# Local attention of a four-layer recurrent network: 1/sqrt as exp of minus half a logarithm, value projections and the next row's shift placed earlier in a step

## The reference, cut to what matters

```
h = shift_token(x)
q, k, v = split(h @ wqkv)
q = l2norm(q) * qs
k = l2norm(k) * ksc
q, k = rotary_xpos(q, k)
o = local_attention(q, k, v)
x = x + o @ wo
```

## Time and profile before

| | us |
|---|---|
| median of 3 runs | 2914.24 |
| lowest, highest | 2912.70, 2918.39 |
| the profiled execution, its time | 2911.34 |
| its span in the trace | 2909.5 |
| PE busy | 2305.2 (79%) |
| DVE busy | 1535.6 (53%) |
| ACT busy | 1138.6 (39%) |
| POOL busy | 637.8 (22%) |
| mean granted TensorE clock | 0.885 |

### The profile page before, as it was taken

The page is one execution under the profiler, slowest core; times in us unless marked ns, Lnnn a source line. Parts: engine busy times, 40 slices in busy tenths (PEclk is TensorE's granted clock), DMA queues, the critical chain, the costliest instruction groups (busy, mean ns, idle before and its releaser), DMA issues. The chain is left out here.

```text
span 2909.5 us, 54198 instructions
## 1 busy us (share of the span) xinstructions
PE 2305.2 (79%) x18107; PEld 1476.4 (51%) x18108; DVE 1535.6 (53%) x5386; ACT 1138.6 (39%) x1810; POOL 637.8 (22%) x689
## 2 busy tenths in 40 slices
PE   4487999997699999784888828447888866999997
PEld 1133777773267777431444416324554313777775
DVE  4635666635466665435677313147775245565663
ACT  5623554433244544333555402133554340233333
POOL 0204434300244342002010040421110012221210
PEclk8796999998899999896999869767999865899999
DMA  2000000000000000001222140202221002333330
GB/s 109 0 0 1 1 1 0 0 1 0 0 1 2 0 0 1 1 4 45 70 80 67 55 150 0 62 28 81 73 74 33 0 33 90 92 111 91 91 110 30
DMA packets 81241, 115.82 MB, mean 40 GB/s; under 512 B 10352, under 2 KB 67184, under 8 KB 77720
## 3 DMA queue, kind: packets, MB, share of 16 engines
q1 hardware_dynamic: 79024, 109.48, 12.4%
q0 software_dynamic: 2048, 4.20, 0.5%
HBM read 69.70 MB, written 42.86 MB: 39 GB/s over the span
## 5 line engine op out<-in xcount | busy, mean ns | idle before, releaser
L1240 ACT ACTIVATE at_pr<-ps 128x768 f32<-128x768 f32 x384 | 312.1, 813 | 505.7 <-PE ps L1176 505.7
L1282 DVE CUSTOM_DVE_ANT_0 at_junk<-ps,conf 128x128 f32<-128x128 f32 x768 | 220.1, 287 | 235.7 <-PE ps L1158 216.0
L1284 DVE CUSTOM_DVE_ANT_0 at_junk<-ps,conf 128x256 f32<-128x256 f32 x768 | 321.4, 419 | 0.0
L1158 PE MATMUL ps<-at_ks,at_qs 40*128 40x128 f32 (+5 forms) x2048 | 223.0, 321 | 70.7 <-DVE at_m L1284 26.9
L1170 PE MATMUL ps<-at_qs,at_ks 41*128 41x256 f32 (+5 forms) x2048 | 199.5, 294 | 58.2 <-DMA at_qs<-at_ml 28.4
L693 POOL TENSOR_TENSOR la_tc<-la_ta,la_tb 128x512 f32<-128x512 f32 x128 | 162.3, 1268 | 354.6 <-DVE la_tb L959 354.6
L710 PE MATMUL ps<-w_l0f,la_hs 128*128 128x512 f32 x256 | 152.5, 680 | 54.4 <-POOL la_hs L675 36.3
L1170 PEld LDWEIGHTS ps<-at_qs,at_ks 41*128 41x128 f32 (+2 forms) x2048 | 140.9, 145 | 105.9 <-ACT at_pr L1240 53.5
L860 ACT ACTIVATE la_pr<-ps 128x640 f32<-128x640 f32 x128 | 90.2, 705 | 265.8 <-PE ps L762 265.4
L1191 PE MATMUL ps<-at_pr,at_v 128*32 128x256 f32 (+1 forms) x3072 | 175.8, 341 | 16.4 <-issue 15.7
L1158 PEld LDWEIGHTS ps<-at_ks,at_qs 40*128 40x128 f32 (+2 forms) x2048 | 104.9, 151 | 160.3 <-DVE at_m L1284 59.2
(11 more groups left out here) (308 smaller groups left out, 4995.6 us busy)
## 6 DMA issues: line engine op xcount, KB each, us to landing
scratch_latent<-at_parts SPq DMA_DIRECT2D x32, 640.0 KB, 4.8
at_qs<-scratch_latent SPq DMA_DIRECT2D x32, 320.0 KB
at_ks<-scratch_latent SPq DMA_DIRECT2D x32, 320.0 KB
scratch_alibi<-at_parts SPq DMA_DIRECT2D x32, 192.0 KB, 2.3
at_ks<-scratch_alibi SPq DMA_DIRECT2D x192, 32.0 KB
scratch_rope<-at_parts SPq DMA_DIRECT2D x32, 192.0 KB, 2.3
at_ks<-scratch_rope SPq DMA_DIRECT2D x192, 32.0 KB
moe_weights<-in_moe SPq DMA_DIRECT2D x1, 4096.0 KB, 20.7
```

The lines of the kernel that those rows point to most:

```text
L1158: m = nc.tensor.matmul(o[:, cols:cols + keys], q[:, block_q:block_q + P], kk[:, 0:keys], start=True, stop=True)
L1240: nc.scalar.activation(pr[:, p % RING, :, :], ps[:, 6:8, 0:384], ACT.Exp, scale=scale).then_inc(s.at_prob, 1)
L1282: nc.vector.tensor_tensor_reduce(junk[:, x % 2, e, 0:P], ps[:, m + e, 0:P], k.cf("late")[:, P:2 * P], 1.0, BIG, ALU.add, ALU.max, m2[:, r, ...
L1284: last_max = nc.vector.tensor_tensor_reduce(junk[:, x % 2, e, P:3 * P], ps[:, m + e, P:3 * P], k.cf("late"), 1.0, BIG, ALU.add, ALU.max, m ...
```

## The change

`y1`, the first estimate of 1/sqrt(vc), is no longer one Abs_reciprocal_sqrt but two activations on ACT in the same place: Ln of `vc` into a new tile `lv`, then Exp with scale -0.5, which waits for the Ln. In each step, `project_values` runs in quarters 0 and 1, and `turn` in quarters 2 and 3, on PE, with ACT's copies out of bank 2 and the semaphore counts to match. `shift_in` of the next row runs on POOL in quarter 2. DVE's part is unchanged.

```diff
@@ -645,6 +645,7 @@
         qn = sb("qn", [P, 2, TILE])
         ss = sb("ss", [P, 4, H8])
         vc = sb("vc", [P, 4, H8])
+        lv = sb("lv", [P, 4, H8])
         y1 = sb("y1", [P, 4, H8])
         y2 = sb("y2", [P, 4, H8])
         rn = sb("rn", [P, 4, H8])
@@ -692,7 +693,7 @@
                         pool.wait_ge(s.la_rot, u + 1)
                         nc.gpsimd.tensor_tensor(tc[:, x, :], ta[:, x % 2, :], tb[:, x % 2, :], ALU.add).then_inc(s.la_tc, 1)
                         pool.wait_ge(s.la_tc, u + 1)
-                    if live(i, -1) and x == 3:
+                    if live(i, -1) and x == 2:
                         if live(i, 2):
                             pool.wait_ge(s.la_vprod, 2 * (row0 + i - 1))
                         shift_in(i + 1, (n + 1) % NS)
@@ -778,7 +779,8 @@
                 m.then_inc(s.la_attended, 1)
 
             def project_values(i, n, t):
-                at_least(pe, s.la_turned, 2 * (row0 + done(i - 1, 4)) + (1 if t and live(i, 4) else 0))
+                at_least(pe, s.la_turned, 2 * (row0 + done(i - 1, 4)))
+                at_least(pe, s.la_vread, 2 * (row0 + i - 2) + t)
                 pe.nop(nofuse=True)
                 nc.tensor.matmul(ps[:, 2, :], hs[:, n, t * P:(t + 1) * P], w("wv"), start=True, stop=True
                                  ).then_inc(s.la_vprod, 1)
@@ -786,7 +788,7 @@
             def turn(i, half):
                 b = row0 + i - 4
                 pe.wait_ge(s.la_divided, 4 * b + 2 * (half + 1))
-                at_least(pe, s.la_vread, 2 * (row0 + done(i - 1, 2)) + (half + 1 if live(i, 2) else 0))
+                at_least(pe, s.la_vread, 2 * (row0 + done(i, 2)))
                 at_least(pe, s.la_turned, 2 * b + half)
                 pe.nop(nofuse=True)
                 for c in range(2):
@@ -831,10 +833,10 @@
                         columns_of(i - row1, (x - 1) % 4)
                     if live(i, 0):
                         product(i, n, x)
-                    if live(i, 2) and x in (0, 2):
-                        project_values(i, (n - 2) % NS, x // 2)
-                    if live(i, 4) and x in (1, 3):
-                        turn(i, x // 2)
+                    if live(i, 2) and x in (0, 1):
+                        project_values(i, (n - 2) % NS, x)
+                    if live(i, 4) and x in (2, 3):
+                        turn(i, x - 2)
                     row = 3 + (x < 3)
                     if live(i, row):
                         values(i - row, (n - row) % NS, (x - 3) % 4)
@@ -861,7 +863,9 @@
                                              ).then_inc(s.la_prob, 1)
                     if live(i, 1) and x == 0:
                         act.wait_ge(s.la_clamped, b)
-                        nc.scalar.activation(y1[:], vc[:], ACT.Abs_reciprocal_sqrt).then_inc(s.la_rsqrt, 1)
+                        nc.scalar.activation(lv[:], vc[:], ACT.Ln).then_inc(s.la_ln, 1)
+                        act.wait_ge(s.la_ln, b)
+                        nc.scalar.activation(y1[:], lv[:], ACT.Exp, scale=-0.5).then_inc(s.la_rsqrt, 1)
                     row1 = 1 + (x < 1)
                     if live(i, row1):
                         p = (x - 1) % 4
@@ -876,14 +880,14 @@
                         act.wait_ge(s.la_product, 4 * b + x + 1)
                         at_least(act, s.la_ss, 4 * b + x - 1)
                         nc.scalar.activation(sq[:, x % 2, :], ps[:, 0, :], ACT.Square).then_inc(s.la_squared, 1)
-                    if live(i, 2) and x in (0, 2):
-                        act.wait_ge(s.la_vprod, 2 * (b - 2) + x // 2 + 1)
+                    if live(i, 2) and x in (0, 1):
+                        act.wait_ge(s.la_vprod, 2 * (b - 2) + x + 1)
                         if live(i, 2 + NS):
                             at_least(act, s.la_attended, HP8 * (b - 1 - NS))
-                        nc.scalar.copy(V[:, (n - 2) % NS, x // 2, :, 0:D64], heads(ps[:, 2, :])).then_inc(s.la_vread, 1)
-                    if live(i, 4) and x in (1, 3):
-                        c = x - 1
-                        act.wait_ge(s.la_turn, 2 * (b - 4) + x // 2 + 1)
+                        nc.scalar.copy(V[:, (n - 2) % NS, x, :, 0:D64], heads(ps[:, 2, :])).then_inc(s.la_vread, 1)
+                    if live(i, 4) and x in (2, 3):
+                        c = 2 * (x - 2)
+                        act.wait_ge(s.la_turn, 2 * (b - 4) + x - 1)
                         at_least(act, s.la_out, b - 4)
                         nc.scalar.copy(oT[:, c:c + 2, :].rearrange("p c t -> p (c t)"), ps[:, 2, :]).then_inc(s.la_turned, 1)
                     if live(i, 3) and x == 1:
@@ -2009,6 +2013,7 @@
         self.la_rot = new("la_rot")
         self.la_tc = new("la_tc")
         self.la_clamped = new("la_clamped")
+        self.la_ln = new("la_ln")
         self.la_rsqrt = new("la_rsqrt")
         self.la_norm = new("la_norm")
         self.la_qn = new("la_qn")
```

## The result

| | before | after |
|---|---|---|
| median, us | 2913.47 (4 runs) | 3008.55 (4 runs) |
| lowest to highest | 2911.65 to 2918.39 | 3007.27 to 3012.20 |
| profiled execution | 2911.34 | 3007.91 |
| its span | 2909.5 | 3006.1 |
| mean granted clock | 0.885 | 0.871 |

The ratio is 1.0326, with a 95% interval of 1.0308 to 1.0344: slower, by 95 us. The forecast had the sign and the mechanism, but 2974 us and a range up to 3000; the measured time lies 8.6 us above the range.

The account below looks back on a forecast made before the run. A step was taken as PE's work plus its waits, with ACT's chain through `y1` on the path in quarter 0. 2911.3 + 40 - 4 + 25 = 2972, with half of a 2.9 us median offset 2974 us; range 2944 to 3000.

Parts of the forecast that it names:

- Part one, Ln and Exp: ACT in quarter 0: two table loads ahead of `y1` make the chain 1.54 us longer in 26 steps, +40.0 us.
- What is saved in quarter 1: ACT's table load ahead of the exp of quarter 1 goes away, but it was hidden, so it gives nothing.
- Part two: POOL's shift in quarter 2: 0 in steady steps, 0.7 us gained at each of six starts, -4 us.
- Part three: Bank 2's order, projection and turn changing quarters on PE: 0, bounds -0.24 to +0.5 us a step.
- The clock: PE's quarter-0 stall of 2.5 us lowers the clock in 6 of 10 steps, 1.6 us each: +25 us, at most +42.
- The third rival: Two loads in quarter 0, and the clock falls in nearly every step and for longer: 2990 to 3030 us, chance 0.10.

Follow-up runs that it names:

- e2: The kernel before with only Ln and Exp in place of Abs_reciprocal_sqrt: 3004.22 us, ratio 1.0305 against the kernel before.
- e4: The changed kernel with eleven unused matmuls added on PE ahead of its wait for `la_ot`: 2960.07 us, ratio 1.0139 against the kernel before.
- e1: The changed kernel with Abs_reciprocal_sqrt back in place of Ln and Exp: 2915.49 us, ratio 1.0006 against the kernel before.
- e3: The changed kernel with one table set holding Ln and Exp loaded ahead of each local attention: 2870.03 us, ratio 0.9833 against the kernel before.
- e6: The changed kernel with Abs_reciprocal_sqrt back and DVE's quarter-0 divide ahead of the inverse norms: 2861.80 us, ratio 0.9838 against the kernel before.
- e8: The kernel before with only DVE's quarter-0 divide moved ahead of the inverse norms: 2886.37 us, ratio 0.9898 against the kernel before.
- e5: The changed kernel, Ln and Exp kept, with DVE's quarter-0 divide ahead of the inverse norms: 2900.26 us, ratio 0.9948 against the kernel before.

## Why the prediction was wrong in its size

By its own steps:

- **Part one, Ln and Exp: right.** Two loads ahead of `y1`, 32 under each line, 1.54 us longer, 26 steps. Where the clock held, the steps show this term by itself: 26.39 and 26.47 us in two steps of e2, 26.3 to 26.4 in e4, as the sum had them. 26 x 1.54 = 40 us stands.
- **What is saved in quarter 1: right**, nothing: e2 without a fall is those 1.54 us longer although the load of quarter 1 is gone.
- **Part two, -4 us: near.** From the first square to the first steady exp the changed kernel took 67.5 and 68.2 us, before 69.8 and 68.1: 2 us less in all. The shift's effect on the stall was under-priced: PE's product now runs on from the transposes, so the projection ended 0.7 us earlier and not 0.44, and the stall is 2.8 us where I had 2.5.
- **Part three, 0: right as far as the runs show.** e1 has the new order of bank 2 and the earlier shift, and its steps without a fall are as long as before. The two parts were tried only together.
- **The clock, +25 us: this step failed.** Between the first and the last quarter-0 exp of the two applications the changed kernel took 404.4 and 399.7 us, before 351.6 and 351.7, 100.8 more; 40 of it is part one, 61 the clock. The term was `26 x 0.6 x 1.6`, and both factors were too small. The share of stalls with a fall was 26 of 26, not 6 of 10: I had set one stall of 2.35 us against one of 2.15, two single stalls of which neither comes back in each step; e1 had the second one again and the clock fell there. And a fall costs 1.7 us only in 15 of 26: in 11 the clock stayed at 0.50 for 6.8 us instead of 3.4, and the step grew by 3.3. 15 x 1.7 + 11 x 3.3 = 62. My upper bound of +42, "all, at 1.6", wasn't one. The third rival, a fall in nearly every step and for longer, is what happened; I had given it 0.10 and cut the range at 3000 inside it.

Sum with what was measured: 2911.3 + 40 + 61 - 2 = 3010, beside 3007.9.

The Trainium skill's rule on the load ("ScalarE: Activation LUTs", table sets: ln then exp in one load) is true of the chip here and false of this program: one set does serve both, as e3 shows, but the loads that the build places by itself didn't choose it. The trace of before had said so in the earlier trace rows.

## What to carry to other kernels

Before swapping an activation for others "of the same table", look in the trace what the build loads for such a pair, and place the shared set by hand if it doesn't; then count the loads again. Ask which wait an in-order engine puts between two chains that have nothing to do with each other: here DVE's divide stood behind `y1` without reading it, and with the two blocks exchanged one load a row no longer costs anything that shows (e6, e8), and a second load costs 1.0 us a step (means of 24.36 in e5 and 23.33 in e6) where in the old order it cost 3.9 (28.80 in the changed kernel, 24.87 before). And where a change lengthens a stall of PE that comes back every step, price the clock as the worse case for all of them. Here that would have been 3.3 us for each of the 26, 86 us, where 61 were lost.

## What the runs showed of the hardware

Of the changed kernel's 26 low spells of the clock in steps 4 to 16, 15 lasted 3.4 us and 11 lasted 6.8, and which of the two went with when the fall came: the 6.8 us ones began from 0.14 us before the stall's end to 0.50 after, the 3.4 us ones 0.62 us after it or later. After a stall of 1.3 us the clock fell in 7 of 24 cases (e1), after 24 of 0.4 to 0.9 never (before). In the lower spell, values' fp32 matmuls of 128x65 went from 0.39 to 0.63 us a pair, the product's from 1.02 to 2.08. And useless work was worth having: eleven matmuls a step that nobody reads saved 48 us (e4).
